# Attention and mixture of experts: V strips and row-sum strips of two steps in one group, a third probabilities buffer, and a token list made by matmuls

## The chip, the cores and the metric

The kernel runs on one core of a Trainium2 chip. The metric is the device time in microseconds of one execution. TensorE multiplies matrices, ScalarE applies functions, VectorE and GpSimd work elementwise, and SyncE (SP) issues transfers. In the profile they are PE (with PEld for its weight loads), ACT, DVE, POOL and SP. SBUF is the memory on the core, PSUM the accumulators of TensorE.

## The reference

The input x has 4 sequences of 1024 tokens with 512 channels. Everything is float32.

```python
q, k, v = (x @ w.T + b, split into 16 heads of 32)
probs = softmax(q @ k.T / sqrt(32))
x = layernorm(x + (probs @ v) @ wo.T + bo)
scores = x @ gate_w.T                       # 8 experts
ew, ei = top_k(scores, 2); ew = softmax(ew)
routed = sum over the two of ew * ((silu(x @ w_gate[e].T) * (x @ w_up[e].T)) @ w_down[e].T)
shared = (silu(x @ sh_gate.T) * (x @ sh_up.T)) @ sh_down.T
x = layernorm(x + routed + sigmoid(x @ se_gate_w.T) * shared)
```

## The kernel before, in words

**Attention.** One sequence is a batch, b of 4; three run in a loop and the last is written out. A batch has 4 groups of 4 heads, and a group has 16 steps: two halves of the queries (512 each) times 8 tiles of keys. `loc` counts the 64 steps of a batch. A step has 4 slots, one for each head. In slot h of step `loc` TensorE computes the scores of step `loc + 1` for head h (`scores`, L549) into a ring of two PSUM banks (`RING`), and ScalarE takes their exponential (`exps`, L683) into a buffer of `probs`. There are two such buffers, chosen by `loc % 2`. At the end of each step TensorE multiplies the probabilities by V (`weighted`, L560): four matmuls with 32 weight columns each, one for each head, which run side by side in the array. These are called strips here. The row sums of the softmax come from `acc`, the sum of the probabilities of two steps (`FOLD`): GpSimd adds the pairs of three heads (L469), VectorE that of the fourth (L795, `FOLD_DVE = 1`), and at every odd step TensorE sums them over partitions with strips (`row_sums`, L574). An exponential waits until its buffer has been multiplied and added.

**Side work.** Each slot also has work for groups further on, given by `side_plan`. "pre" is one of 64 preliminary score matmuls of the next group (L532), of which VectorE takes a row maximum (L765); they use three PSUM banks in a ring. "proj" is one of 16 pieces of the K and Q projection of the group after next: three float32r matmuls of high and low parts (L499). Piece i stands in slot `PROJ_FROM + PROJ_UNIT * (i // 4) + PROJ_EVERY * (i % 4)`, so the last one is in slot 53 of 64. After every fourth piece ScalarE copies the high half (`high`, L663), and VectorE makes the low half ("low", L754) two slots later. "row" sends the maxima back as an extra row of the stacked K and Q.

**Queues.** Each engine works in the order in which the code gives it instructions. SP goes through `body` for each group: inverting row sums, `row` for the first half, weights (`load_w`), for group 1 the next batch's x (`load_x`), `spread`, and `row` for the second half. `spread` (L279) waits for all four low halves of a projection and copies K and Q into `kq_stack` with 12 transfers, three for each head. GpSimd's loop (`batch`) folds at each odd step, normalises at steps 9 and 11, and at step 13 (`SPLIT_W_AFTER`) it first waits for the complete projection and then splits the next weights, which use the same buffer:

```python
if at == SPLIT_W_AFTER and not (last and g > 0):
    projected(b * G + g + 2)      # pool.wait_ge(proj_ready, PROJ * (n + 1))
    split_w(b * G + g + 3)
```

In group 1, step 15 and group 2, steps 1, 3 and 5 it also splits two chunks each of the next x. After a batch come the V tiles of the next batch (`v_tile`, L499, which read `wv_hi` and `wv_lo`) and the output tiles (`o_tile`, L591) with their layernorm. The result x2 goes to memory.

**Feed-forward.** `scores` computes the router. `feed_forward` then has 32 tiles of 128 tokens for the shared expert. The first 12 (`COVER`) run while the routing is worked out; their code is written out, without a loop. VectorE ranks the chosen experts (`first_choice`, `second_choice`, `count`, `positions`). Then GpSimd scatters each token's number to its place in a table in memory, with 64 indirect transfers of 128 numbers of 4 bytes (L1321), and SP reads the table back into `who_all` after the base of tile 9. GpSimd gathers the tokens of 72 expert tiles by it (L1331), one after the other. The other 20 shared tiles and the combination follow.

Of the kernel before, what the change touches and what calls it, by code (L numbers as in the profile page):

```python
# [5 lines left out]
ALU = mybir.AluOpType  # L6
ACT = mybir.ActivationFunctionType
AX = mybir.AxisListType
F32 = mybir.dt.float32
# [24 lines left out]
PROJ_FROM, PROJ_EVERY, PROJ_UNIT = 2, 3, 14  # L34
# [6 lines left out]
FOLD_DVE = 1  # L41
# [46 lines left out]
def attention(nc, x, xT, wkqT, wvT, woT, bq, bk, bv, bo, x2, passed):  # L88

    inv_rows = nc.dram_tensor("inv_rows", (HG, HALF), F32, kind="Internal").ap()  # L90

    with ExitStack() as ctx:
# [16 lines left out]
        wv_hi = sb("wv_hi", [P, C, D], F32R)  # L109
        wv_lo = sb("wv_lo", [P, C, D], F32R)  # L110
# [14 lines left out]
        probs = sb("probs", [P, 2, HG, HALF])  # L125
# [11 lines left out]
        x_nat = probs[:].rearrange("p a h d -> p (a h) d")  # L137
# [47 lines left out]
        wo_in = sem("wo_in")  # L185
        few_in = sem("few_in")
# [14 lines left out]

        def res_of(t):

            return x_nat[:, t - 2, :] if 2 <= t < 6 else res[:, t % 2, :]
# [43 lines left out]
        def _(sp):  # L248
# [62 lines left out]
            def body(b, m, g, last):  # L311
# [57 lines left out]
            spread(0, 0)  # L369
            row(-1, -1, 0, False)  # L370
# [15 lines left out]
        def _(pool):  # L386
# [71 lines left out]
            def fold(b, loc):  # L458

                i, j = loc // FOLD, loc % FOLD  # L460
                for h in range(FOLD_POOL):
# [5 lines left out]
                    if j > 1:  # L467
                        pool.wait_ge(folded, (b * FOLDS + folds(loc) - 2) * FOLD_POOL + h + 1)
                    nc.gpsimd.tensor_tensor(acc[:, h, :], probs[:, (loc - 1) % 2, h, :] if j == 1 else acc[:, h, :],  # L469
                                            probs[:, loc % 2, h, :], ALU.add).then_inc(folded, 1)  # L470
# [24 lines left out]
        def _(pe):  # L495
# [57 lines left out]
            def weighted(b, loc):  # L553
# [5 lines left out]
                for h in range(HG):  # L559
                    done = nc.tensor.matmul(ps_ctx[h * HD:(h + 1) * HD, :],  # L560
                                            v_sb[:, kt, (g * HG + h) * HD:(g * HG + h + 1) * HD],
                                            probs[:, loc % 2, h, :], start=kt == 0, stop=kt == KT - 1)
# [32 lines left out]
            def batch(b, last):  # L595
                for loc in range(BSTEPS):
                    g = loc // STEPS
                    for slot in range(SLOTS):
                        if loc + 1 < BSTEPS:
                            scores(b, loc + 1, slot)  # L600
                        if loc == 0 and slot < SIDE_RING:
                            pe.wait_ge(tail_free, b * TAIL + KT - (2 - slot if slot < 2 else 0) - (slot < 2))
# [25 lines left out]
            with pe.Fori(0, B - 1) as b:  # L628
                batch(b, False)
                pe.wait_ge(side_free, base_of(b * G + G))  # L630
                for t in range(KT):
                    v_tile(b * TAIL + KT + t, t, ps_side[:, t % TAIL_RING, :], TAIL_RING)
                pe.wait_ge(wo_in, 16 * (b + 1))
                for t in range(KT):
                    if t % (KT // NHALF) == 0:
                        pe.wait_ge(ctx_done, (b + 1) * G * NHALF - (t == 0))
                    o_tile(b * TAIL + 2 * KT + t, t, ps_side[:, (KT + t) % TAIL_RING, :],
# [1251 lines left out]
```

## Time and profile before

| | |
|---|---|
| median of 3 runs | 2303.1 us (2297.88 to 2305.36) |
| the profiled execution | 2299.8 us |
| its span, first to last instruction | 2298.1 us |
| mean granted clock of TensorE | 0.972 |
| PE busy | 2130.9 us, 93% |
| PEld busy | 1177.7 us, 51% |
| DVE busy | 1212.6 us, 53% |
| ACT busy | 851.8 us, 37% |
| POOL busy | 953.1 us, 41% |
| attention: first strips of V, first output tile of the last batch | 92.24 us, 1392.71 us |
| shared tiles under the routing | 1494.15 us to 1671.48 us |

Times of instructions count from the start of the span. Busy is the time in which an engine has an instruction at work. A matmul's record is longer than its share of the array, since matmuls overlap, so the distance between starts says what one costs. The granted clock is given as a share of the full 2.4 GHz, and 0.50 is the lower level of 1.2 GHz. Idle time is put down to what ended it; "issue" means that the profile shows nothing that the engine waited for.

### The profile page before, as it was taken

The numbers are of one execution on the slowest core, as the hardware profiler recorded it, in microseconds if no ns is written. First come the engines' busy times: TensorE is split into PE (matmuls) and PEld (weight loads), VectorE is DVE, ScalarE is ACT, GpSimd is POOL, SyncE is SP. The second block draws the span as 40 slices with busy tenths as digits, with TensorE's granted clock in tenths as the row PEclk, the third lists the DMA queues.
The fourth block names the chain that finished last, engine by engine and source line by source line (L and its number), as shares of the span: only waits on it lengthen the run. The fifth ranks groups of instructions, "written<-read, shape, count | busy, mean of one in ns | idle before, by whom it ended". The sixth has DMA issues, their size and how long they took to land. (4 is left out here: it accounts for less than half of the span.)

```text
span 2298.1 us, 34596 instructions
## 1 busy us (share of the span) xinstructions
PE 2130.9 (93%) x9524; PEld 1177.7 (51%) x9525; DVE 1212.6 (53%) x2169; ACT 851.8 (37%) x1508; POOL 953.1 (41%) x926
## 2 busy tenths in 40 slices
PE   7999999999999999999999986791899999999997
PEld 5544445445445445445555422470754444445886
DVE  6767665567665566665567723450222222223875
ACT  2355553355553355554355662320111111111332
POOL 1245753454753454754454564427021111112651
PEclk9999999999999999999999998895999999999999
DMA  4230333221433221333221303560132222223762
GB/s 137 65 71 29 94 70 89 80 61 30 100 68 93 80 48 42 98 70 76 95 55 26 75 11 111 197 256 0 53 105 90 91 90 84 90 91 116 228 184 77
DMA packets 96850, 202.83 MB, mean 88 GB/s; under 512 B 26912, under 2 KB 27424, under 8 KB 94752
## 3 DMA queue, kind: packets, MB, share of 16 engines
q1 hardware_dynamic: 83744, 165.04, 24.6%
q0 software_dynamic: 12928, 35.70, 5.7%
q8 instruction: 78, 1.28, 0.2%
q14 instruction: 100, 0.82, 0.1%
HBM read 110.68 MB, written 39.13 MB: 65 GB/s over the span
## 5 line engine op out<-in xcount | busy, mean ns | idle before, releaser
L765 DVE TENSOR_REDUCE max_half<-ps_side 128x1 f32<-128x512 f32 x1024 | 663.5, 683 | 335.4 <-PE ps_side L532 326.1
L683 ACT ACTIVATE probs<-ps_s 128x512 f32<-128x512 f32 x1024 | 573.4, 596 | 485.9 <-PE ps_s L549 391.2
L469 POOL TENSOR_TENSOR acc<-probs 128x512 f32<-128x512 f32 x384 | 484.7, 1289 | 486.5 <-ACT probs L683 480.8
L549 PE MATMUL ps_s<-kq_stack 97*128 97x512 f32 x1024 | 461.5, 454 | 23.5 <-ACT probs L683 14.4
L532 PE MATMUL ps_side<-kq_stack 96*128 96x512 f32 x1024 | 399.8, 401 | 10.9 <-DVE max_half L765 7.2
L549 PEld LDWEIGHTS ps_s<-kq_stack 97*128 97x128 f32 x1024 | 192.6, 189 | 361.0 <-ACT probs L683 222.3
L560 PE MATMUL ps_ctx<-probs,v_sb 128*32 128x512 f32 x2048 | 274.5, 608 | 0.0
L1433 PE MATMUL ps_gu<-gu_sb,xT_e 128*128 x576 | 261.3, 596 | 0.5 <-issue 0.3
L1331 POOL DMA_INDIRECT x_g<-x,who_all x72 | 67.8, 941 | 389.0 <-PE ps_t L1423 325.7
L532 PEld LDWEIGHTS ps_side<-kq_stack 96*128 96x128 f32 x1024 | 195.9, 191 | 44.9 <-DVE max_half L765 13.8
L1433 PEld LDWEIGHTS ps_gu<-gu_sb,xT_e 128*128 128x128 f32 x576 | 103.7, 190 | 107.7 <-issue 107.3
L1541 ACT ACTIVATE act_g<-ps_gu 128x256 f32<-128x256 f32 x72 | 27.6, 383 | 351.3 <-PE ps_gu L1433 351.3
L1618 DVE TENSOR_TENSOR hid<-act_g,ps_gu 128x256 f32<-128x256 f32 x72 | 30.3, 421 | 224.6 <-ACT act_g L1541 224.6
L1456 PE MATMUL ps_d<-wd_sb,act_g 128*128 x288 | 135.6, 593 | 0.5 <-DVE act_g L1625 0.5
L574 PE MATMUL ps_sum<-acc,ones 128*32 128x512 f32 x1024 | 133.5, 593 | 2.7 <-POOL acc L469 1.4
L795 DVE TENSOR_TENSOR acc<-probs 128x512 f32<-128x512 f32 x128 | 105.7, 826 | 36.8 <-ACT probs L683 36.8
L499 PE MATMUL ps_side<-x_hi,wkq_hi 128*128 128x512 f32 x256 | 103.9, 406 | 15.3 <-DVE x_lo L838 10.7
L1375 PE MATMUL ps_gu<-sgu_hi,xT_hi 128*128 128x512 f32 x256 | 105.0, 410 | 12.8 <-issue 10.4
L499 PE MATMUL ps_side<-x_hi,wkq_lo 128*128 128x512 f32 x256 | 102.3, 400 | 0.0
L499 PE MATMUL ps_side<-x_lo,wkq_hi 128*128 128x512 f32 x256 | 102.0, 399 | 0.0
L1375 PE MATMUL ps_gu<-sgu_hi,xT_lo 128*128 128x512 f32 x256 | 101.7, 397 | 0.3 <-issue 0.3
L1375 PE MATMUL ps_gu<-sgu_lo,xT_hi 128*128 128x512 f32 x256 | 101.5, 396 | 0.0
(194 smaller groups left out, 2477.5 us busy)
## 6 DMA issues: line engine op xcount, KB each, us to landing
kq_stack<-kq SPq DMA_DIRECT2D x192, 256.0 KB, 5.1
y_slots<-y_t SPq DMA_DIRECT2D x72, 256.0 KB, 2.3
res<-inv_rows SPq DMA_DIRECT2D x128, 64.0 KB, 2.0
probs<-x SPq DMA_DIRECT2D x16, 512.0 KB, 5.1
x_r<-x SPq DMA_DIRECT2D x32, 256.0 KB, 3.7
x_t<-x SPq DMA_DIRECT2D x32, 256.0 KB
gu_sb<-wgu SPq DMA_DIRECT2D x8, 1024.0 KB, 14.9
out<-gu_sb SPq DMA_DIRECT2D x32, 256.0 KB, 2.6
```

Of the source, the lines that this page charges most:

```text
L469: nc.gpsimd.tensor_tensor(acc[:, h, :], probs[:, (loc - 1) % 2, h, :] if j == 1 else acc[:, h, :], probs[:, loc % 2, h, :], ALU.add).then_ ...
L499: done = nc.tensor.matmul(out, w, m, start=first and i == 0, stop=last and i == 2)
L532: nc.tensor.matmul(bank, q_stack[par][0:3 * HD, h, t * P:(t + 1) * P], k_stack[par][0:3 * HD, h, half * HALF:(half + 1) * HALF], start=Tru ...
L549: nc.tensor.matmul(ps_s[:, (loc * HG + h) % RING, :], k_stack[par][0:3 * HD + 1, h, kt * P:(kt + 1) * P], q_stack[par][0:3 * HD + 1, h, ha ...
L560: done = nc.tensor.matmul(ps_ctx[h * HD:(h + 1) * HD, :], v_sb[:, kt, (g * HG + h) * HD:(g * HG + h + 1) * HD], probs[:, loc % 2, h, :], s ...
L574: done = nc.tensor.matmul(ps_sum[h * HD:(h + 1) * HD, :], ones[:], acc[:, h, :], start=kt == FOLD - 1, stop=kt == KT - 1)
L683: nc.scalar.activation(probs[:, loc % 2, h, :], ps_s[:, (loc * HG + h) % RING, :], ACT.Exp, scale=HD ** -0.5).then_inc(probs_ready, 1)
L765: nc.vector.reduce_max(max_half[:, u // 2, u % 2:u % 2 + 1], bank, AX.X).then_inc(side_free, 1)
L795: nc.vector.tensor_tensor(acc[:, h, :], probs[:, (loc - 1) % 2, h, :] if j == 1 else acc[:, h, :], probs[:, loc % 2, h, :], ALU.add).then_ ...
L1375: done = nc.tensor.matmul(out, w, m, start=c == 0 and i == 0, stop=c == last_c and i == 2)
L1433: done = nc.tensor.matmul(ps_gu[:, s % 2, :], e_xT[:, s % 2, c, :], gu_sb[:, bass.ds(e, 1), c, :].rearrange("p a n -> p (a n)"), start=c = ...
L1456: done = nc.tensor.matmul(ps_d[:, s % 2, :], e_hT[:, s % 2, c, :], wd_sb[:, bass.ds(e, 1), c, :].rearrange("p a n -> p (a n)"), start=c == ...
```

## The change

Four things are changed together.

1. `weighted` for both steps of a pair and `row_sums` run one after the other at the end of the odd step. A third probabilities buffer, `probs_mid`, takes the steps with `loc % 3 == 1`; an exponential waits for the V strips and the row sums that read its buffer three steps before.
2. `probs_mid` lies on top of `wv_lo` in SBUF. So `wv_lo` is copied to memory once at the start (`wv_lo_kept`), and SP loads it again (1 MB) in the last group of each batch but the last. The V tiles wait for this.
3. GpSimd adds the pairs of all four heads (`FOLD_DVE = 0`), VectorE none. The projection pieces stand in slots 0, 4, 8, ..., 60. The PSUM banks of the tail's tiles are shifted by one.
4. The token table is no longer scattered to memory. VectorE makes one-hot tiles of each token's row in its tile (`in_tile`, 128 columns) and of its tile's number times the token's number (`of_tile`, 72 columns), in 8 parts after tiles 3 to 6. TensorE multiplies them in 64 f32 matmuls that accumulate in `ps_who`, after tiles 4 to 7, and VectorE copies the result to `who_all`.

```diff
-PROJ_FROM, PROJ_EVERY, PROJ_UNIT = 2, 3, 14
+PROJ_FROM, PROJ_EVERY, PROJ_UNIT = 0, 4, 16
-FOLD_DVE = 1
+PROBS = 3
+FOLD_DVE = 0
...
+        with nc.sbuf_tensor("probs_mid", [P, HG, HALF], F32) as probs_mid:
+            pass
         wv_lo = sb("wv_lo", [P, C, D], F32R)
...
+        def probs(loc, h):
+            return probs_mid[:, h, :] if loc % PROBS == 1 else probs_outer[:, loc % PROBS // 2, h, :]
...
+        def tail_bank(i):
+            return ps_side[:, (i + SIDE_RING) % TAIL_RING, :]
         def res_of(t):
-            return x_nat[:, t - 2, :] if 2 <= t < 6 else res[:, t % 2, :]
+            return probs_mid[:, t - 2, :] if 2 <= t < 6 else res[:, t % 2, :]
...
         # SP, body(), after spread
+                if not last and g == G - 1:
+                    sp.wait_ge(pv_done, (b + 1) * BSTEPS - FOLD)
+                    sp.wait_ge(sum_done, (b + 1) * SUMS - 1)
+                    sp.sem_inc(passed_sp, 1)
+                    sp.dma_start(wv_lo[:].bitcast(F32), wv_lo_kept).then_inc(wv_moved, 16)
...
         # SP, at the start
             spread(0, 0)
+            sp.wait_ge(wv_split, C)
+            sp.dma_start(wv_lo_kept, wv_lo[:].bitcast(F32)).then_inc(wv_moved, 16)
...
         # PE, batch()
-                        if slot == SLOTS - 1:
-                            weighted(b, loc)
-                            if loc % FOLD == FOLD - 1:
-                                row_sums(b, loc)
+                        if slot == SLOTS - 1 and loc % FOLD == FOLD - 1:
+                            for done in range(loc - FOLD + 1, loc + 1):
+                                weighted(b, done)
+                            row_sums(b, loc)
...
         # PE, ahead of the V tiles
+                pe.wait_ge(wv_moved, 16 * (b + 2))
...
         # ACT, exps()
-                if loc >= 2:
-                    act.wait_ge(pv_done, b * BSTEPS + loc - 1)
-                    if h < FOLD_POOL:
-                        act.wait_ge(folded, (b * FOLDS + folds(loc - 2) - 1) * FOLD_POOL + h + 1)
-                    else:
-                        act.wait_ge(folded_dve, (b * FOLDS + folds(loc - 2) - 1) * FOLD_DVE + h - FOLD_POOL + 1)
+                if loc >= PROBS:
+                    act.wait_ge(pv_done, b * BSTEPS + loc - PROBS + 1)
+                    act.wait_ge(sum_done, b * SUMS + (loc - PROBS) // FOLD + 1)
...
         # feed_forward
+TABLE_PARTS = 8
+PART = 2 * TT // TABLE_PARTS
+COUNT_COLUMNS_AFTER = 3
+TABLE_AFTER = {3: (0, 1), 4: (2, 3), 5: (4, 5), 6: (6, 7)}
+LOOK_UP_AFTER = {4: (0, 1), 5: (2, 3), 6: (4, 5), 7: (6, 7)}
+WHO_AFTER = 7
...
-            for t in range(TT):
-                for v in range(2):
-                    nc.gpsimd.indirect_dma_start(
-                        table, bass.IndirectOffsetOnAxis(ap=col_i[4][:, v, t:t + 1].bitcast(U32), axis=0),
-                        token[:, t:t + 1], None).then_inc(scattered, 16)
...
+            def look_up(part):
+                pe.wait_ge(part_made, part + 1)
+                for c in range(PART):
+                    done = nc.tensor.matmul(ps_who, in_tile[:, part % 2, c, :], of_tile[:, part % 2, c, :],
+                                            start=part == 0 and c == 0, stop=part == TABLE_PARTS - 1 and c == PART - 1)
+                done.then_inc(part_read, 1)
...
+            def table_part(part):
+                k, first = part * PART // TT, part * PART % TT
+                if part == 0:
+                    dve.wait_ge(columns_made, 1)
+                    link(v.tensor_copy(columns, ps_count))
+                if part >= 2:
+                    dve.wait_ge(part_read, part - 1)
+                v.tensor_tensor(in_tile[:, part % 2], rows[:, 0, k, first:first + PART].unsqueeze(2).broadcast_to((P, PART, P)),
+                                columns.unsqueeze(1).broadcast_to((P, PART, P)), ALU.is_equal)
+                for c in range(PART):
+                    t = first + c
+                    done = v.tensor_scalar(of_tile[:, part % 2, c, :], columns[:, 0:NT], rows[:, 1, k, t:t + 1],
+                                           col[0][:, t:t + 1], ALU.is_equal, ALU.mult)
+                done.then_inc(part_made, 1)
```

## Rows read from the trace of the kernel before

**Rows 1.** Groups of instructions by line: busy, mean ns, idle before by releaser.
```profile
L683 ACT ACTIVATE probs<-ps_s 128x512 f32<-128x512 f32 x1024 | 573.4, 596 | 485.9 <-PE ps_s L549 391.2 <-DVE acc L795 33.9 <-POOL acc L469 23.6
```

**Rows 2.** Timeline of TensorE, last batch's last group: start, us, instruction, idle before.
```profile
1345.58 1.07 PE L560 MATMUL ps_ctx<-probs,v_sb 128*32 128x512 f32 x8
1346.47 1.04 PE L574 MATMUL ps_sum<-acc,ones 128*32 128x512 f32 x8
1347.44 0.73 PE L549 MATMUL ps_s<-kq_stack 97*128 97x512 f32 x2
...
1349.55 1.07 PE L560 MATMUL ps_ctx<-probs,v_sb 128*32 128x512 f32 x8
1350.54 0.73 PE L549 MATMUL ps_s<-kq_stack 97*128 97x512 f32 x2
1351.73 0.99 PE L549 MATMUL ps_s<-kq_stack 97*128 97x512 f32 x2 [0.45 <-ACT probs L683]
1352.65 0.64 PE L560 MATMUL ps_ctx<-probs,v_sb 128*32 128x512 f32 x4
```

**Rows 3.** Timeline of TensorE: first V strips of groups 1 and 2, third batch.
```profile
861.47 1.06 PE L560 MATMUL ps_ctx<-probs,v_sb 128*32 128x512 f32 x8
...
934.67 1.06 PE L560 MATMUL ps_ctx<-probs,v_sb 128*32 128x512 f32 x8
```

**Rows 4.** Timeline of all engines at the end of group 1, second batch.
```profile
572.11 0.97 POOL L403 CAST wkq_hi<-stage 128x512 fp32r<-128x512 f32 x1 [1.12 <-PE ps_side L499]
...
576.33 3.75 POOL L469 TENSOR_TENSOR acc<-probs 128x512 f32<-128x512 f32 x3
...
578.04 0.50 PE L549 MATMUL ps_s<-kq_stack 97*128 97x512 f32 x1
...
580.41 1.07 PE L560 MATMUL ps_ctx<-probs,v_sb 128*32 128x512 f32 x8
```

**Rows 5.** Timelines at the first batch's end; DMA issues: KB each, us to landing.
```profile
374.23 13.78 SPq L279 DMA_DIRECT2D kq_stack<-kq  x12
...
377.08 0.49 PE L532 MATMUL ps_side<-kq_stack 96*128 96x512 f32 x1
...
380.80 0.50 PE L499 MATMUL ps_side<-wv_hi,x_hi 128*128 128x512 f32 x1
381.13 0.40 PE L499 MATMUL ps_side<-wv_hi,x_lo 128*128 128x512 f32 x1
381.37 0.40 PE L499 MATMUL ps_side<-wv_lo,x_hi 128*128 128x512 f32 x1
...
kq_stack<-kq SPq DMA_DIRECT2D x192, 256.0 KB, 5.1
...
acc<-woT SPq DMA_DIRECT2D x3, 1024.0 KB, 5.0
```

**Rows 6.** Windows (busy by engine, PEclk, DMA share, GB/s), timeline; second batch's start.
```profile
438.00:444.00 6.00, 6.00 (x17) 3.22 (x18) 3.65 (x6) 1.19 (x2) 3.46 (x3) 0.50 0.01 4
...
441.54 0.60 ACT L683 ACTIVATE probs<-ps_s 128x512 f32<-128x512 f32 x1 [5.03 <-POOL acc L469]
```

**Rows 7.** Shared tiles: scatter's line, TensorE's timeline, DMA queues 1549 to 1600, window.
```profile
L1321 POOL DMA_INDIRECT table<-token,col_i x64: 954/958/1236, 1532.2 to 1612.0; - x64
...
1549.32 0.60 PE L1369 MATMUL ps_t<-ident_m,x_t 128*128 128x128 f32 x4
1551.37 0.47 PE L1375 MATMUL ps_d<-sd_hi,hT_hi 128*128 128x512 f32 x1 [1.45 <-issue]
...
1613.67 0.76 PE L1375 MATMUL ps_gu<-sgu_hi,xT_hi 128*128 128x512 f32 x1 [10.14 <-issue]
...
1659.65 0.60 PE L1369 MATMUL ps_t<-ident_m,x_t 128*128 128x128 f32 x4
...
1663.20 0.48 PE L1375 MATMUL ps_gu<-sgu_hi,xT_hi 128*128 128x512 f32 x1
...
q0 software_dynamic: 1312, 0.02, 1.9%
q1 hardware_dynamic: 143, 0.26, 1.7%
...
1614.00:1672.00 58.00, 57.00 (x261) 46.30 (x261) 15.99 (x24) 9.63 (x17) 2.96 (x4) 0.96 0.20 63
```

More of the change, by code:

```diff
@@ L185, in attention @@
         wo_in = sem("wo_in")
+        wv_moved = sem("wv_moved")
         few_in = sem("few_in")
@@ L468, in fold @@
                         pool.wait_ge(folded, (b * FOLDS + folds(loc) - 2) * FOLD_POOL + h + 1)
-                    nc.gpsimd.tensor_tensor(acc[:, h, :], probs[:, (loc - 1) % 2, h, :] if j == 1 else acc[:, h, :],
-                                            probs[:, loc % 2, h, :], ALU.add).then_inc(folded, 1)
+                    nc.gpsimd.tensor_tensor(acc[:, h, :], probs(loc - 1, h) if j == 1 else acc[:, h, :],
+                                            probs(loc, h), ALU.add).then_inc(folded, 1)
             def batch(b, last):
@@ L794, in fold @@
                         dve.wait_ge(folded_dve, (b * FOLDS + folds(loc) - 2) * FOLD_DVE + h - FOLD_POOL + 1)
-                    nc.vector.tensor_tensor(acc[:, h, :], probs[:, (loc - 1) % 2, h, :] if j == 1 else acc[:, h, :],
-                                            probs[:, loc % 2, h, :], ALU.add).then_inc(folded_dve, 1)
+                    nc.vector.tensor_tensor(acc[:, h, :], probs(loc - 1, h) if j == 1 else acc[:, h, :],
+                                            probs(loc, h), ALU.add).then_inc(folded_dve, 1)
             def batch(b, last):
@@ L1100, in feed_forward @@
 def feed_forward(nc, x2, sgu_hi, sgu_lo, sd_hi, sd_lo, wgu, wd, base, y, gu_sb, wd_sb, route, sgate_all, weights, pos,
-                 tile_expert, table, ident, out, passed):
+                 tile_expert, ident, out, passed):
     with ExitStack() as ctx:
@@ L1150, in feed_forward @@
         te = spare[:, 0:NT]
+        columns = spare[:, 3 * NT * E + 4 * TT:3 * NT * E + 4 * TT + P]
+        in_tile = x_g[:].rearrange("p s d -> p (s d)").rearrange("p (i c m) -> p i c m", i=2, c=PART)
+        of_tile = spare[:, NT * E:NT * E + 2 * PART * NT].rearrange("p (i c n) -> p i c n", i=2, c=PART)
         y_g = gu_sb[:, 0:4, 0:2, :]
@@ L1257, in _ @@
                 load_tile(t)
-            sp.wait_ge(made, 5)
-            sp.dma_start(table.rearrange("(p n) a -> p (n a)", p=P), zero_table[:]).then_inc(zeroed, 16)
             for e in range(E):
@@ L1484, in _ @@
                 if t == 1:
-                    pe.wait_ge(made, 6)
+                    pe.wait_ge(made, 5)
                     pe.wait_ge(visits, 1)
@@ L1489, in _ @@
                     nc.tensor.matmul(ps_total, all_ones[:], flat, start=True, stop=True).then_inc(counted, 1)
+                if t == COUNT_COLUMNS_AFTER:
+                    pe.wait_ge(ranked, 1)
+                    nc.tensor.matmul(ps_count, all_ones[:], tri[:], start=True, stop=True).then_inc(columns_made, 1)
+                for part in LOOK_UP_AFTER.get(t, ()):
+                    look_up(part)
             expert_turn(0, 0)
@@ L1760, in positions @@
                 link(v.tensor_copy(rows[:, 1], col_i[1][:]))
-                link(v.scalar_tensor_tensor(out=rows[:, 0], in0=rows[:, 0], scalar=float(NT), in1=rows[:, 1],
-                                            op0=ALU.mult, op1=ALU.add))
-                v.tensor_copy(col_i[4][:], rows[:, 0]).then_inc(placed, 1)
-                dve.wait_ge(placed, 1)
+                link(v.tensor_copy(col[0][:], token[:]))
                 link(v.tensor_tensor(ends, tile_start, end[:].unsqueeze(1).broadcast_to((P, NT, E)), ALU.is_ge))
@@ L1785, in _ @@
                     positions(running)
+                for part in TABLE_AFTER.get(t, ()):
+                    table_part(part)
+                if t == WHO_AFTER:
+                    who()
             finish(COVER - 1)
@@ L1809, in moe @@
     y = nc.dram_tensor("y_slots", (SLOTS_ALL, D), F32, kind="Internal").ap()
-    table = nc.dram_tensor("table", (SLOTS_ALL, 1), I32, kind="Internal").ap()
     with ExitStack() as ctx:
@@ L1837, in moe @@
         feed_forward(nc, x2, sgu_hi, sgu_lo, sd_hi, sd_lo, wgu, wd, base, y, gu_sb, wd_sb, route, sgate_all, weights,
-                     pos, tile_expert, table, ident, out, passed)
+                     pos, tile_expert, ident, out, passed)
 def build(nc, x, xT, wkqT, wvT, woT, bq, bk, bv, bo, shg, shu, shd, rw, wgu, wd, out):
```

65 lines of the change are left out of this document (34 added, 31 removed).

## The prediction, made before the changed kernel was run

> **What bounds the kernel now.** I read the page's busy shares, then the idle time by releaser, then the order of instructions at four places. TensorE is busy 93% of the span, so the attention part (to 1393 us) changes only by what changes TensorE's own stream. ScalarE's exponentials wait for TensorE most of the time, and 33.9 + 23.6 us of their idle time ends with an addition into `acc` [rows 1]. Those waits exist because there are two probabilities buffers. In a group with no side work the stream is: strips of one step 0.99 us (1349.55 to 1350.54), strips of V to strips of row sums 0.89, row sums to the next scores 0.97, and 1.19 us for two scores, because the third score waits for the first exponential (a ring of two banks) [rows 2]. A group with projections takes 73.2 us for 16 steps [rows 3], 9.15 us for two.
>
> The feed-forward part has a hole. From 1532.2 to 1612.0 GpSimd issues the 64 scatters of the token table. From 1551 on TensorE's matmuls come singly, and the one at 1613.67 follows 10.14 us of idle time that nothing in the profile explains [rows 7]. The step after `turn` comes 3.55 us later where nothing disturbs (1659.65 to 1663.20). After the `turn` at 1549.32 it was due at 1552.87, and it came 60.8 us late [rows 7].
>
> **The change, part by part.**
>
> *Strips of two steps in one group.* An exit from strips costs 0.99 − 0.89 = 0.10 us, and one of two goes. But ScalarE can work off only two exponentials during a strip group, so the ring of two now paces eight scores in a row instead of twice four. In a bare group: three rounds of 1.19, then 0.92 from the last round to the strips (1351.73 to 1352.65), then 0.89 + 0.89 + 0.97, which is 7.24 us against 7.07 for the pair from 1345.58 to 1352.65 [rows 2]: a loss of 0.17. With projections: 22 matmuls at 0.24 (381.13 to 381.37 [rows 5]) are 5.2, the first after strips adds 0.1 (0.33 instead of 0.24 [rows 5]), strips 2.75. Slots without a projection piece last 0.48 on TensorE and about 0.6 in the ring; I take 0.3 a step for what the slot with a piece doesn't give back, and 0.3 a pair for the copy of a finished projection, which pushes exponentials back. Sum 8.95, against 9.05 (9.15 less the one wait for `kq_stack` in that group, estimated at 1.1 over eight pairs). So −0.1 on 112 pairs: **−11 us**. Bounds: ring free, −0.95 a pair, −106; the bare group's +0.17 on all 128, +22. I stay near the middle rows because rounds of 1.19 stand in the trace with nothing else waited for. The 57.5 us of ScalarE's waits [rows 1] are inside this term.
>
> *GpSimd adds four heads.* Three additions take 3.75 us [rows 4], 1.25 each, so four take 5.0 of a pair's 9: hidden, unless GpSimd starts late. It does at the end of each group. `PROJ_FROM, PROJ_EVERY, PROJ_UNIT` = 0, 4, 16 moves the last projection piece from slot 53 to slot 60. GpSimd's `projected` ahead of `split_w` waits for it, and the fold of steps 14 and 15 is queued behind. Count from the score of slot 60 (578.04 [rows 4]): the piece ends at +1.4, the split lasts 4.2 (572.11 to 576.33), four additions 5.0: sums ready at +10.7. TensorE's strips started at +2.37 (580.41); a piece (0.7) and the copy (0.2) more give +3.3, two V strips 1.76: row sums wanted at +5.1. TensorE stands for **5.6 us**, and ScalarE's `take` and the next scores' exponentials stand with it. This happens where `split_w` follows and no larger wait covers it: groups 0 to 2 of three batches and group 0 of the last, 10 × 5.6 = **+56** (bounds 4.5 and 6.5 each). Before, three additions were ready in time.
>
> *Clock.* After the idle time at a batch's start the granted clock was 0.50 from 438 to 444 [rows 6], the lower level, 1.2 GHz. After each 5.6 us I take some 3.4 us at that level, half of which is lost: 10 × 1.7 = **+17** (bounds 0 and 34).
>
> *The reload of `wv_lo`.* It is behind `spread` in SP's queue. `spread` now waits for the low half at slot 62: copy and subtraction after the piece bring it to +3.1 after slot 60, where before it started before slot 60 (374.23 against 377.08). Its 12 transfers take SP 13.8 us, so the reload is issued at +17. The last transfers land about 5.1 us after their issue, and 1 MB lands 5.0 after its own on quiet queues [rows 5]: between +22 and +25, taken +23.5. TensorE reached the first V tile at +3.7 (380.80); with a second step's strips it is +4.6. It waits 18.9 us, three times: **+57**, and +2 each for the clock, **+6**. The row sums' wait of that group lies under it. The inversion of the last row sums and the loads of x follow the reload in SP's queue, but the V tiles (96 matmuls at 0.24) take 23 us and start late as well, so they stay covered; if not, it costs a few us a batch.
>
> *`spread` elsewhere.* Its first head lands 6.5 after the start (1.4 for three issues, 5.1 to land), at +9.6; the next group's first preliminary scores want it at +6.4. Where the row sums wait it is hidden; the last batch's group 1 pays 3, and in group 1 of the others it is behind `load_x`, which waits for the split: 1 each. **+6.** *x splits:* pairs with four additions and two split chunks (5.0 + 4.2 + gaps) need 9.4 on GpSimd against 8.95, in four pairs of three batches: **+6** (0 to 15). *Batch start:* the first strips and the wait of 5.03 us on `acc` at 441.54 [rows 6] go, while TensorE's wait for VectorE after its loop turns stays: **−7** (0 to −12). *Prologue:* the same later last piece, and the copy of `wv_lo` out: **+3** (0 to 8).
>
> *Token list by matmuls.* The scatters go, the hole with them: 60.8, plus 3.4 for the slow matmuls after it and 0.6 in the next step: **−65**. The price is 64 f32 matmuls of two passes. The nearest row is four transposes of 128 columns in 0.60, the last alone 0.27, so 0.11 a pass: 128 × 0.11 = **+14**, on TensorE's path (bounds: 8, if columns alone count, and 31 at the 0.24 of a 512-column matmul). VectorE was busy 16 of 58 us in this stretch at 0.67 an instruction [rows 7], so its new work, some 3 us a part and two parts a tile, lies beside TensorE's 9.1 + 3.5. At 0.67 for each narrow one too it would show, by up to 13 us.
>
> Against this stands a rule. No packet of an instruction queue is among those of 1549 to 1600 [rows 7]. By the Trainium skill, Runtime: NRT & Kernel Launch, "Instruction fetch mechanics", fetching is mostly hidden in code without taken branches, and this stretch is unrolled; the trace agrees that no fetch was under way. By that rule removing scatters cures no lack of instructions, and unless they block something else the hole would stay.
>
> **Sum.** −11 + 56 + 17 + 57 + 6 + 6 + 6 − 7 + 3 = +133 in attention; −65 + 14 = −51 after it; together +82 on the profiled execution's 2299.8, 2382. The median of the runs is 3.3 above that execution: **2385 us**.
>
> **The rivals.**
> 1. *The ring costs nothing* (the other side). If TensorE's path in a pair is only its matmuls, a pair is 8.1, −95 more: 2290. It decides when the eight scores lose under 0.1 us a pair to exponentials. For it: ScalarE is busy 37%. Against: the rounds of 1.19 [rows 2] don't depend on that share.
> 2. *The row sums don't wait*: the fold of four is ready by +5.1. Then 56 and 17 go and `spread` shows at nine more ends, +27: 2339. Against: the order in GpSimd's queue.
> 3. *The hole stays*, being no effect of the scatters: 2450. Against: it lies inside them and ends with them.
> 4. *The reload is covered* (it lands by +4.6, ahead of the spread): −63, 2322. Against: the queue's order.
>
> **How the numbers follow.** Forecast 0.70, with its own range 2335 to 2430; rival 1: 0.11; rival 2: 0.08; rival 3: 0.05; rival 4: 0.06. The range of 8 in 10 runs from 2318 to 2435: it takes in rivals 2 and 4 and leaves out 1 and 3. A difference of 0.3% is what a measurement of this kernel can tell. Slower 0.85; faster 0.11, nearly all of it rival 1; within 0.3% 0.04, between rivals 1 and 4.
>
> **What would show it.** A wait of the row sums' matmuls on `acc` of 5 to 6 us at 10 group ends; waits of the first V tiles for `wv_lo`, three of nearly 19 us; a granted clock below 1 after both; score waits for exponentials in nearly every pair; a closed hole in the feed-forward part, with 0.1 us for each pass of the look-up. The forecast is wrong if waits at group ends stay under 2 us, if the reload lands before the strips end, or if GpSimd's four additions take much more than 5.0 and every pair waits for them.

## The result and the profile after

The changed kernel took 2373.8 us, the median of four runs from 2370.0 to 2385.5, against 2303.4 for the kernel before: a ratio of 1.032 (interval 1.028 to 1.036). It is slower by 70 us where 82 were forecast. Its profiled execution spans 2372.0 us at a mean granted clock of 0.954, where before had 2298.1 and 0.972.

I read the waits of TensorE first. Columns: engine and line, what it waited for, us in total, times, the longest.

```profile
PE ps_sum L595 <- POOL acc L490: 73.7, 14, 6.2
PE ps_side L520 <- DMA wv_lo<-wv_lo_kept: 38.7, 3, 13.2
PE ps_s L570 <- ACT probs_outer L705: 20.9, 52, 0.8
...
PE ps_s L570 <- ACT probs_mid L705: 11.5, 26, 0.8
...
PE ps_side L553 <- DMA kq_stack<-kq: 6.5, 2, 3.9
```

The first two rows are the two waits of the forecast: 14 on GpSimd's additions (ten of 5.3 us at the group ends, three of 6.15 at the batch ends and one of 2.2 at the end of the last batch) and 3 on the reload. The scores' waits for exponentials are 78, 32.4 us in all; the forecast looked for one in nearly every pair, and from 99 to 1316 us, 104 pairs, there are 49. Before, ScalarE's exponentials had 485.9 us of idle time ahead of them, 33.9 and 23.6 of it for an addition into `acc` [rows 1]. After, the view of the exponentials' line gives what ended their idle time (us, times):

```profile
its engine sat idle before it (us, times) until:
  PE ps_s L570: 409.3, 291
  issue: 0.9, 3
```

No addition is among the releasers. What is left is waiting for TensorE, and making it shorter would not make TensorE's own work shorter. Here is why the row sums wait: GpSimd's timeline at the end of group 1 of the second batch, which answers to [rows 4].

```profile
619.89 0.61 POOL L424 CAST wkq_hi<-stage 128x512 fp32r<-128x512 f32 x1 [6.62 <-PE ps_side L520]
...
622.49 1.27 POOL L426 TENSOR_TENSOR wkq_lo<-stage,wkq_hi 128x512 fp32r<-128x512 f32 x1
623.72 4.91 POOL L490 TENSOR_TENSOR acc<-probs_outer,probs_mid 128x512 f32<-128x512 f32 x4
```

TensorE's timeline of the same place, with the last projection piece at its head:

```profile
618.78 0.40 PE L520 MATMUL ps_side<-x_hi,wkq_hi 128*128 128x512 f32 x1
...
621.44 1.06 PE L581 MATMUL ps_ctx<-probs_outer,v_sb 128*32 128x512 f32 x8
622.32 1.04 PE L581 MATMUL ps_ctx<-probs_mid,v_sb 128*32 128x512 f32 x8
628.69 1.94 PE L595 MATMUL ps_sum<-acc,ones 128*32 128x512 f32 x8 [5.32 <-POOL acc L490]
```

GpSimd has been idle for 6.62 us when the last piece lets it go on; then the split and the four additions follow, and the row sums start 0.06 us after the last addition (623.72 + 4.91). The fold has nothing to do with the piece; it is only queued behind the split that waits for it. The row-sum matmuls take 1.94 instead of 1.04 us, because the clock fell during the wait (windows; columns after the length are PE, PEld, DVE, ACT and POOL busy, the granted clock, DMA share and GB/s):

```profile
620.00:624.00 4.00, 2.56 (x19) 0.67 (x18) 1.04 (x3) 2.50 (x5) 3.84 (x5) 1.00 0.20 60
624.00:632.00 8.00, 3.31 (x11) 1.18 (x12) 0.00 (x0) 1.11 (x3) 7.84 (x8) 0.65 0.82 184
```

At the first batch's end, [rows 5] before, SP's queue and then TensorE's:

```profile
396.16 14.13 SPq L293 DMA_DIRECT2D kq_stack<-kq  x12
410.93 0.66 SPq L346 DMA_DIRECT2D wv_lo<-wv_lo_kept  x1
```

```profile
403.40 1.94 PE L595 MATMUL ps_sum<-acc,ones 128*32 128x512 f32 x8 [6.15 <-POOL acc L490]
418.59 0.79 PE L520 MATMUL ps_side<-wv_hi,x_hi 128*128 128x512 f32 x1 [13.24 <-DMA wv_lo<-wv_lo_kept]
```

The reload is issued once the 12 transfers of `spread` are out, and it lands 7.6 us after its issue. TensorE stands for 6.15 + 13.24 = 19.4 us at this batch end, and about as long at the other two (the three waits for `wv_lo` are 38.7 us in all), and from 402 to 422 us it had half its clock:

```profile
402.00:422.00 20.00, 5.35 (x17) 2.95 (x18) 0.00 (x0) 0.60 (x1) 1.35 (x2) 0.51 0.83 218
```

How long the groups are can be read from the first V strips of groups 0, 1, 2 and 3 of the third batch and of group 0 of the last batch:

```profile
862.88 0.64 PE L581 MATMUL ps_ctx<-probs_outer,v_sb 128*32 128x512 f32 x4
941.35 0.64 PE L581 MATMUL ps_ctx<-probs_mid,v_sb 128*32 128x512 f32 x4
1020.01 1.06 PE L581 MATMUL ps_ctx<-probs_outer,v_sb 128*32 128x512 f32 x8
1098.41 0.64 PE L581 MATMUL ps_ctx<-probs_outer,v_sb 128*32 128x512 f32 x4
1241.03 1.06 PE L581 MATMUL ps_ctx<-probs_outer,v_sb 128*32 128x512 f32 x7
```

Group 1 takes 78.7 us where it had 73.2 [rows 3]. Group 0 takes 78.5 us, and the group that ends the batch 142.6 us with V and output tiles. Before, these two took 72.2 and 123.2 us, from the V strips of the second step of groups 0, 1 and 3 and of the last batch's group 0 (the second step, because it is the one that ends a pair):

```profile
793.05 0.64 PE L560 MATMUL ps_ctx<-probs,v_sb 128*32 128x512 f32 x4
...
865.24 1.06 PE L560 MATMUL ps_ctx<-probs,v_sb 128*32 128x512 f32 x8
...
1013.51 0.64 PE L560 MATMUL ps_ctx<-probs,v_sb 128*32 128x512 f32 x4
...
1136.67 0.64 PE L560 MATMUL ps_ctx<-probs,v_sb 128*32 128x512 f32 x4
```

A pair of the last group, without projections ([rows 2] before: 7.07 us):

```profile
1465.14 1.92 PE L581 MATMUL ps_ctx<-probs_outer,v_sb 128*32 128x512 f32 x16
1466.91 1.06 PE L595 MATMUL ps_sum<-acc,ones 128*32 128x512 f32 x8
1467.91 0.73 PE L570 MATMUL ps_s<-kq_stack 97*128 97x512 f32 x2
1469.09 0.99 PE L570 MATMUL ps_s<-kq_stack 97*128 97x512 f32 x2 [0.45 <-ACT probs_outer L705]
1470.28 0.99 PE L570 MATMUL ps_s<-kq_stack 97*128 97x512 f32 x2 [0.19 <-ACT probs_outer L705]
1471.46 1.00 PE L570 MATMUL ps_s<-kq_stack 97*128 97x512 f32 x2 [0.19 <-ACT probs_outer L705]
1472.39 1.06 PE L581 MATMUL ps_ctx<-probs_mid,v_sb 128*32 128x512 f32 x8
```

From strips to strips it takes 7.25 us, with three score rounds of 1.19 in a row, as worked out ahead. In the feed-forward part the hole is closed: TensorE has no idle time from 1673 to 1740 us (window below). The look-up's 128 passes come in four sets of 32. With such a set the next matmul follows 3.93 us after the transposes (1666.88 to 1670.81), where without one it follows after 0.35 (run 9, 1553.32 to 1553.67): 3.58 us a set, 0.11 us a pass.

```profile
1666.88 0.60 PE L1418 MATMUL ps_hts<-ident_m,hid 128*128 128x128 f32 x4
1667.32 3.69 PE L1483 MATMUL ps_hts<-y_t,x_g 128*128 128x72 f32 x32
1670.81 0.48 PE L1393 MATMUL ps_gu<-sgu_hi,xT_hi 128*128 128x512 f32 x1
```

```profile
1673.00:1740.00 67.00, 67.00 (x369) 57.38 (x368) 30.87 (x70) 10.12 (x18) 4.04 (x4) 1.00 0.20 63
```

The first output tile of the last batch comes at 1519.07 us against 1392.71: +126.4 for attention (+133 forecast). The profiled execution is longer by 2373.8 − 2299.8 = 74.0, so −52.4 is left for everything after (−51 forecast).

### The profile page after: what moved, and what is told of

Read it like the earlier page. It is cut to its first block and busy times, and to the rows that moved or that the text cites. A ratio compares the mean times of both kernels' runs of the same rounds, so it can differ in the third digit from the quotient of the medians.

```text
span 2372.0 us, 34378 instructions
## 1 busy us (share of the span) xinstructions
PE 2149.6 (91%) x9654; PEld 1216.2 (51%) x9655; DVE 1140.7 (48%) x2114; ACT 854.6 (36%) x1508; POOL 1036.6 (44%) x989
## 5 line engine op out<-in xcount | busy, mean ns | idle before, releaser
L787 DVE TENSOR_REDUCE max_half<-ps_side 128x1 f32<-128x512 f32 x1024 | 648.4, 683 | 457.7 <-PE ps_side L553 450.3
L705 ACT ACTIVATE probs_outer<-ps_s 128x512 f32<-128x512 f32 x688 | 389.1, 596 | 289.1 <-PE ps_s L570 268.6
L553 PE MATMUL ps_side<-kq_stack 96*128 96x512 f32 x1024 | 404.9, 407 | 14.4 <-DVE max_half L787 7.7
L490 POOL TENSOR_TENSOR acc<-probs_outer,probs_mid 128x512 f32<-128x512 f32 x176 | 220.2, 1282 | 123.0 <-ACT probs_mid L705 116.9
L490 POOL TENSOR_TENSOR acc<-probs_outer 128x512 f32<-128x512 f32 x176 | 220.0, 1280 | 116.7 <-ACT probs_outer L705 116.7
L490 POOL TENSOR_TENSOR acc<-probs_mid,probs_outer 128x512 f32<-128x512 f32 x160 | 200.4, 1284 | 117.2 <-ACT probs_outer L705 117.2
L705 ACT ACTIVATE probs_mid<-ps_s 128x512 f32<-128x512 f32 x336 | 191.0, 596 | 149.3 <-PE ps_s L570 140.7
L595 PE MATMUL ps_sum<-acc,ones 128*32 128x512 f32 x1024 | 146.4, 646 | 73.7 <-POOL acc L490 73.7
L581 PE MATMUL ps_ctx<-probs_outer,v_sb 128*32 128x512 f32 x1376 | 177.0, 610 | 0.0
L595 PEld LDWEIGHTS ps_sum<-acc,ones 128*32 128x32 f32 x1024 | 32.4, 114 | 157.7 <-POOL acc L490 96.0
```

Of the source, the lines that this page charges most:

```text
L490: nc.gpsimd.tensor_tensor(acc[:, h, :], probs(loc - 1, h) if j == 1 else acc[:, h, :], probs(loc, h), ALU.add).then_inc(folded, 1)
L553: nc.tensor.matmul(bank, q_stack[par][0:3 * HD, h, t * P:(t + 1) * P], k_stack[par][0:3 * HD, h, half * HALF:(half + 1) * HALF], start=Tru ...
L581: done = nc.tensor.matmul(ps_ctx[h * HD:(h + 1) * HD, :], v_sb[:, kt, (g * HG + h) * HD:(g * HG + h + 1) * HD], probs(loc, h), start=kt == ...
L595: done = nc.tensor.matmul(ps_sum[h * HD:(h + 1) * HD, :], ones[:], acc[:, h, :], start=kt == FOLD - 1, stop=kt == KT - 1)
L705: nc.scalar.activation(probs(loc, h), ps_s[:, (loc * HG + h) % RING, :], ACT.Exp, scale=HD ** -0.5).then_inc(probs_ready, 1)
L787: nc.vector.reduce_max(max_half[:, u // 2, u % 2:u % 2 + 1], bank, AX.X).then_inc(side_free, 1)
```

## The experiments

Each was timed beside the kernel before on its own chip. The first four ran on a chip where the kernel before took 2301.2 us (median of 11), the other eight on one where it took 2246.2 and 2246.0 us (23 and 16 runs). Which chip the runs of the result were made on isn't on record; their times and the hole in the trace of before are those of the first of these two, and they are counted with it. What makes the two chips differ became a question of its own (runs 7 and 9 to 12).

**1. The fold ahead of the split.** The split moves behind the last pair's fold.

```diff
-NORM_AFTER, SPLIT_W_AFTER = (11, 9), 13
+NORM_AFTER, SPLIT_W_AFTER = (11, 9), 15
```

> The changed kernel with the weights' split moved from step 13 to step 15 of a group, so that GpSimd adds the last pair before it waits for the projection piece of slot 60. My theory (the order in GpSimd's queue makes the row sums wait): the ten waits of 5.3 us on acc go; what then shows is spread's late landing, which the last batch's group 1 shows already (last pair 12.6 us there, 16.1 where the row sums wait, 8.8 with neither). So 3.6 us at ten ends, about -36: 2338 us, with waits on kq_stack of 3 to 4 us in place of those on acc, and the first V tiles' wait for wv_lo longer by 6 us. Rival (four additions on GpSimd are simply too much work, whatever their order): the row sums still wait, some 2374 us.

Measured: 2366.0 us, ratio 1.029 (1.026 to 1.032), so 8 us less than the change and not 36. The cause was right and the gain was not. The waits of TensorE:

```profile
PE ps_side L520 <- DMA wv_lo<-wv_lo_kept: 59.7, 3, 20.3
PE ps_side L553 <- DMA kq_stack<-kq: 51.5, 12, 8.6
```

No row sum at the end of a group with projections waits for `acc` any more. But the next group's first preliminary score now waits for `spread`, and the whole of the batch end's 20 us is a wait for the reload. At the first group end (TensorE's timeline):

```profile
164.26 0.50 PE L570 MATMUL ps_s<-kq_stack 97*128 97x512 f32 x1
167.59 0.50 PE L553 MATMUL ps_side<-kq_stack 96*128 96x512 f32 x1 [2.83 <-DMA kq_stack<-kq]
```

In group 1 that wait is longer than the one it replaces, because SP issues x loads ahead of `spread` there, and they wait for the split, which now comes later still (the first batch's group 1):

```profile
248.26 0.79 PE L553 MATMUL ps_side<-kq_stack 96*128 96x512 f32 x1 [8.30 <-DMA kq_stack<-kq]
```

So the first batch's group 1 became 3.5 us longer than in the changed kernel (81.9 against 78.4), while its groups 0 and 2 became 2.9 and 3.3 shorter (V strips to V strips in the two traces). The three waits lie one above the other, and all three start later because the last projection piece is in slot 60. For the reload that is the smaller part, as run 2 shows.

**2. The reload ahead of `spread`** in SP's queue (in `body`).

```diff
+                if not last and g == G - 1:
+                    ...
+                    sp.dma_start(wv_lo[:].bitcast(F32), wv_lo_kept).then_inc(wv_moved, 16)
                 if not (last and g >= G - 2):
                     spread(m + 2, g % 2, m, ...)
```

> The changed kernel with the reload of wv_lo ahead of spread in SP's queue (it still waits for the strips of step 61). My theory (the reload is late because it is queued behind spread's 12 transfers): the three waits of V tiles (13.2 us each) go, and with them some 4 us each at the lower clock; the row sums' wait of that end stays. -17 a batch, -51: 2323 us. Rival (the reload is late because of its own length, or its wait for the strips): V tiles still wait over 5 us each, 2350 or more.

Measured: 2334.1 us, ratio 1.015 (1.012 to 1.017). The wait for `wv_lo` is gone from the list, the one on `acc` is unchanged at 73.7 us, and the change loses 40 of its 70 us. The reload was late by the order in the queue, not by its 1 MB, and not by the projection piece, which stood in slot 60 here too. The expected 2323 was missed by 11 us: it had 51 us for the three waits, and they gave 40.

**3. Both together.**

> Both moves together. My theory: neither wait is left at the batch ends, -19 each, and -36 at the ten other group ends: 2281 us, 1% faster than the kernel before, all of it from the token list. Rival (one of the two waits hides a third thing, for instance the row sums' inversion or the loads of x behind spread in SP's queue): the batch ends stay above 75 us and the total above 2300.

Measured: 2308.7 us, ratio 1.0037 (1.0025 to 1.0049). The total stays above 2300, as the rival said, and the expected 2281 was missed by 28 us. Without the reload's wait above it, moving the split is worth 25 us. What is left is the third wait:

```profile
PE ps_side L553 <- DMA kq_stack<-kq: 51.8, 12, 8.6
```

**4. The new token list alone**: attention as before, the feed-forward part as changed.

```diff
-                    nc.gpsimd.indirect_dma_start(
-                        table, bass.IndirectOffsetOnAxis(ap=col_i[4][:, v, t:t + 1].bitcast(U32), axis=0),
-                        token[:, t:t + 1], None).then_inc(scattered, 16)
+LOOK_UP_AFTER = {4: (0, 1), 5: (2, 3), 6: (4, 5), 7: (6, 7)}
```

> The attention part of the kernel before with the feed-forward part of the changed one: the token list by matmuls alone. My theory (the scatters block every engine for some 60 us): -65 for the hole and +14 for 128 passes of 0.11 us, 2252 us (2247 to 2258). Rival (the hole comes from something else in this stretch): it stays, and the look-ups add their 14: 2317 us.

Measured: 2247.9 us, ratio 0.977 (0.975 to 0.979). On this chip the list is worth −53 us, as in the changed kernel, and TensorE has no idle time in the hole's place (window):

```profile
1548.00:1614.00 66.00, 66.00 (x364) 56.57 (x363) 30.20 (x68) 10.12 (x18) 4.04 (x4) 1.00 0.21 64
```

From here on the kernel before takes 2246 us.

**5. The reload first, and the projection pieces in their old slots**, two moves at once, so that all three waits should go. The reload stands ahead of `spread` as in run 2; the second edit is this.

```diff
-PROJ_FROM, PROJ_EVERY, PROJ_UNIT = 0, 4, 16
+PROJ_FROM, PROJ_EVERY, PROJ_UNIT = 2, 3, 14
```

> The changed kernel with the reload of wv_lo ahead of spread and the projection pieces back in their old slots (2, 3, 14: the last in slot 53); the split is at step 13 as before. My theory (all group-end waits come from the piece in slot 60): no wait on acc, on kq_stack or on wv_lo over 1.5 us is left; pairs keep their 8.9 us against 9.05, so attention gains some 15 us, and with the list's 54 the kernel takes 2303 - 54 - 15 + 3 for the start = 2237 us. Rival (four additions and the split are too much for GpSimd at a group's end even so): the row sums wait some 2 us at each end, clock included 2270.

Measured: 2254.4 us, ratio 1.0046 (1.003 to 1.0062). In its trace no V tile waits for the reload of `wv_lo`, preliminary scores wait three times for `kq_stack` (2.8 us in all), and the row sums wait once for `acc`, 2.2 us at the end of the last batch. The 17 us missed are not a matter of the chip: 2303 less the list's 54 is 2249 us, and the list alone took 2247.9 and 2245.8 us on the two chips. What isn't there is the gain of 15 us in attention; run 12 shows where it is lost. No run has the pieces in their old slots with the reload still behind `spread`. By the rows of before, `spread` would then be out at 388.0 us (374.23 + 13.78), the reload would land some 7.5 us later, as it does in the changed kernel, and the V tiles would want it at about 381.7 (380.80 and 0.9 for a second step's strips): a wait of some 14 us, an estimate. So the slot alone would not have cured the reload.

**6. The same with each step's V strips in a group of their own.**

```diff
-                        if slot == SLOTS - 1 and loc % FOLD == FOLD - 1:
-                            for done in range(loc - FOLD + 1, loc + 1):
-                                weighted(b, done)
-                            row_sums(b, loc)
+                        if slot == SLOTS - 1:
+                            weighted(b, loc)
+                            if loc % FOLD == FOLD - 1:
+                                row_sums(b, loc)
```

> As the one with the pieces in the old slots, and besides the strips of each step in a group of their own, as before the change; third buffer, four additions and list stay. It gives what joining two steps' strips is worth. My theory (0.10 to 0.20 us a pair saved on entries and exits, most of it lost again to the ring of two score banks, which gets only two exponentials done under a strip group): within 10 us of the joined one, either side; the third buffer alone gives most of the attention's gain. Rival (joining is worth its full 0.2 us on 128 pairs): 26 us slower than the joined one.

Measured: 2251.5 us, ratio 1.0028 (1.0017 to 1.0038). Merging the strips gains nothing; the version with the strips apart is 0.1% faster, and the intervals overlap. By the traces merging gives 0.4 us in each group 0 (71.6 us in run 5, 72.0 here), and in a bare group it costs (7.25 us a pair, where before had 7.07).

**7. Half the scatters** in the kernel before. This version leaves out the second choice of each token, so it is of use for its times alone.

```diff
-                    sp.wait_ge(scattered, 16 * 2 * TT)
+                    sp.wait_ge(scattered, 16 * TT)
...
-                for v in range(2):
+                for v in range(1):
```

> The kernel before with 32 scatters instead of 64 (the second choice of each token is not entered in the table; the gathers then fetch token 0 for it, at the same sizes). If the scatters block the engines from a point some 14 to 17 of them after the first until the last is issued, the hole ends 32 x 1.26 = 40 us sooner: 2263 us. If the hole is a fixed effect of this stretch, it keeps its 60 us: 2303.

Measured: 2231.2 us, ratio 0.994 (0.992 to 0.996). Neither theory said this: this chip has no hole to halve. The 15 us are another matter, told with run 9.

**8. Pieces every four slots, but 14 slots a unit.**

```diff
-PROJ_FROM, PROJ_EVERY, PROJ_UNIT = 0, 4, 16
+PROJ_FROM, PROJ_EVERY, PROJ_UNIT = 0, 4, 14
```

> The changed kernel with the reload ahead of spread and the pieces in slots 0, 4, 8, 12 of units 14 apart (the last in slot 54). The two end waits depend on the last piece alone, so it should be within 5 us of the one with the old slots: 2237. Rival (evenly spread pieces matter for the ring: a piece in slot 0 of each step gives exponentials time): 10 us or more apart.

Measured: 2377.3 us, ratio 1.058 (1.056 to 1.060), a miss by 140 us. The waits of TensorE:

```profile
PE ps_side L520 <- DVE kq L776: 65.6, 42, 1.8
PE ps_side L520 <- POOL x_lo L426: 26.3, 8, 4.9
```

The last piece of a unit is in slot 12, VectorE makes its low half two slots on, in slot 14, and there the next unit's first piece already wants the bank: 1.6 us, 42 times. Slots 0, 4, 8, 12 of 16 leave room; 2, 5, 8, 11 of 14 as well. The placement of the pieces is a matter of single slots. The two rows are 78 us more than in run 5, of the 123 us between the two runs; the rest isn't accounted for, and a part may be the clock (0.953 granted against 0.981).

**9. The kernel before again, for its trace on this chip.**

> The kernel before, unchanged, for its trace on the chip of this call. On the chip of the second call it took 2246.2 us where the first two calls had 2303.4 and 2301.2, and with half of the scatters 2231.2. If the stretch without tensor work beside the 64 scatters (62.3 us on the first chip) belongs to the chip and not to the program, this trace has it where the time is near 2302 and doesn't have it where the time is near 2246, with all other stretches alike. If it is always there, a time near 2246 must show some 55 us less in other stretches, the attention's above all.

Measured: 2248.8 us. Attention is the same (the last output tile starts at 1422.3 us against 1421.5), and the hole isn't there. Windows, to be read beside those of the kernel before at the same stretch, which follow in a second fence:

```profile
1548.00:1614.00 66.00, 60.08 (x291) 49.60 (x289) 18.52 (x27) 11.32 (x20) 49.94 (x53) 0.99 0.17 49
```

```profile
1548.00:1614.00 66.00, 9.01 (x28) 5.18 (x27) 2.07 (x3) 1.79 (x3) 49.44 (x52) 0.54 0.04 8
```

The scatters are the same in both, 64 from 1533.0 to 1612.8 us at 958 ns here [rows 7 for before]. What does show here is a wait that the hole had hidden: the first expert tile wants its tokens, and they can't be gathered until the last scatter is done and the table read back.

```profile
1621.16 1.12 PE L1423 MATMUL ps_t<-ident_m,x_g 128*128 128x128 f32 x4 [13.08 <-DMA x_g<-x,who_all]
```

With half the scatters, of which the last starts at 1568.5 us, that wait is gone: 15 us less in run 7. The instruction queues among the DMA queues between 1549 and 1600 us in this trace:

```profile
q8 instruction: 2, 0.03, 0.3%
q14 instruction: 2, 0.02, 0.1%
```

In the trace of before the same stretch had no packet of an instruction queue [rows 7]; in that of run 4, on the first chip without scatters, it had three.

**10. The changed kernel again.**

> The changed kernel, unchanged, beside the kernel before on this chip. It has no scatters, so it should take about 2373 us on any chip if the missing hole is what makes the kernel before 57 us faster on the second call's chip: ratio 1.031 where the kernel before takes 2302, 1.057 where it takes 2246. If that chip is faster in other stretches, the changed kernel is faster there too: about 2318 us and a ratio still near 1.03.

Measured: 2376.8 us, ratio 1.058 (1.056 to 1.061), with waits on `acc` of 73.7 us and on `wv_lo` of 38.7 us, as in the trace of the result. The changed kernel is as fast on both chips (2373.8 and 2376.8), and so is the list alone (runs 4 and 11); only the kernel before differs.

**11. The list alone again.**

> The kernel before with the new token list alone (no scatters, look-ups from a table). It took 2247.9 us beside 2301.2. Where the kernel before has its hole: 0.977 again. Where it hasn't: the scatters' own cost is gone, but the look-ups' 14 us are added (four passes of 3.58 us), so within 0.5 per cent of 2246 us, ratio 0.997 to 1.004. If this chip is faster in other stretches, 0.977 on it too, some 2195 us.

Measured: 2245.8 us, ratio 1.0002 (0.9993 to 1.0011). On this chip the list is worth nothing: it saves the 13 us of waiting of run 9 and adds some 14 for the look-up.

**12. Run 5's version beside it.** The edits are those of run 5 and no others.

> The changed kernel with the reload of the weights ahead of the spread, the projection pieces early in each group and the adds begun early (2254.4 us on the second call's chip). It too has no scatters and should take 2250 to 2258 us on any chip; beside the list alone (2247.9 us) it says what the merged strips and GpSimd's adds cost once both waits are gone: some 5 us. If the merged strips are worth their switches (11 us by the prediction), it is the faster of the two.

Measured: 2255.0 us, ratio 1.0038 (1.0023 to 1.0052), 9 us over the list alone. One row of its waits is larger than with the list alone, where `x_lo` costs 5.2 us in six waits:

```profile
PE ps_side L520 <- POOL x_lo L426: 13.4, 6, 3.5
```

It is the stretch in which GpSimd also splits the next x. With four heads to add, it is late. In the traces the groups 2 of the three batches together take 13.3 us more than with the list alone (run 11), of which these waits are 8.2, and the last group takes 6.4 more; the other groups are shorter, by up to 2.1 us. In run 6 the groups 2 are as long (78.8, 78.7 and 79.3 us, against 78.7, 81.2 and 78.1 here and 75.7, 74.2 and 74.8 in run 11), so this is not the work of the merged strips. That it is the fourth addition fits, and no run takes it back by itself.

## Why the prediction was right, and where it wasn't

*The row sums' wait* (10 × 5.6): 5.3 us each, and 6.15 at the three batch ends, where the forecast had counted it under the reload's. From the last piece to the end of the additions the forecast had 9.3 us, and it took 9.0. Run 3 against run 2 prices the order in GpSimd's queue at 25 us net, because `spread` comes next; the prediction's rival 2 had put that cover at 27 of its 73, and it is more like 48 (73 less 25). Run 1 shows the limit of that rival: alone it is worth 8.

*The reload* (57 and 6 for the clock): TensorE stands for 19.4 us at the first batch's end where 18.9 were forecast, and the reload landed 22.4 us after the start of `spread` (20.4 forecast). Run 2 puts its share at 40 us, not 63. The rest is time in which TensorE also waits for the row sums (3 × 6.15), and that wait stays when the reload's goes. So rival 4's price was too high by 23 us; in the sum it makes no difference.

*The clock*: the granted clock falls to its lower level of 1.2 GHz at these waits (0.65 from 624 to 632 us, 0.51 from 402 to 422). The prediction took some 3.4 us at that level after each wait, a choice for which it gave no row. The third batch's group 0 became 6.3 us longer (78.5 against 72.2). Of this 5.3 are the wait; with −0.6 for the strips (next point) 1.6 are the clock (1.7 forecast). The two mean granted clocks, 0.954 and 0.972, would understate it, since the mean of before holds the hole, 66 us at 0.54 in which TensorE had next to nothing to do.

*The strips* (−11, with bounds −106 and +22): the ring does pace eight scores in a row, and the bare pair came out at 7.25 (7.24 forecast). With the waits gone, group 0 of run 12 takes 71.6 us where the list alone has 72.2, −0.6 where −0.8 was forecast. Rival 1 falls. But not all of the 0.6 is the merging: in run 6, with the third buffer and the strips apart, the group takes 72.0. And over the whole kernel run 6 shows no gain: apart is no slower.

*The mis-sized terms*. `x` splits: +6 forecast. In the change's group 2 the next x is split behind longer waits and nothing shows (+3.7 a group, where groups 0 and 1 have +5.3 to +6.3); once these are gone, run 12 waits 8 us more for it than the list alone. The two bare groups at the end stand at nothing in the sum, though the prediction's own 0.17 us a pair would have given 16 pairs 2.7 us. The last one alone has +8.2 to the output tile (0.9 of it because the second step's strips now stand behind the mark from which it is measured). In it the V strips ran twice at half speed, and a window shows the clock at 0.62:

```profile
1479.50:1484.00 4.50, 4.50 (x25) 1.03 (x24) 0.00 (x0) 1.48 (x3) 1.82 (x2) 0.62 0.01 4
```

No wait of note stands ahead of it; the bare group before had 1.00 throughout. What made it fall isn't shown. The sum over attention was 126.4 where 133 were forecast. That it came so close is in part luck. The ten group ends had 65 us of the forecast (5.6 + 1.7 − 0.8 each), or 71 with the x splits, and these groups became 53.5 us longer in the traces; the two bare groups at the end were left out of the sum and became 9.5 us longer.

*The token list* (−65 and +14): on the first chip −52.4 for −51, and the look-up at 0.11 us a pass, as taken. VectorE's new work stayed hidden (31.2 us busy in the 40 from 1660). But one step of this part is wrong in its reason. The prediction said that the hole is made by the scatters. Run 9 shows the same scatters, in the same kernel, without a hole, and run 11 the list then worth nothing. On the first chip the hole goes when the scatters go (run 4), and they aren't enough to make one. So the ratio is 1.032 on one chip and 1.058 on the other, where the change costs 131 us (run 10). The forecast could not have seen it from one trace; that its −65 held is luck of the chip on which the two were timed.

*The row on instruction fetch*: the prediction took the missing instruction packets as a sign that no fetch was wanted. Where nothing is disturbed, the same 51 us have four of them (run 9). None in the hole can as well mean that fetches were wanted and didn't come, with TensorE, VectorE and ScalarE at a stand at the same time. In the trace of before TensorE is idle for 40.0 us at one place and VectorE for 50.4, both with nothing waited for:

```profile
1602.42 1.11 PE L1400 MATMUL ps_hts<-ident_m,hid 128*128 128x128 f32 x4 [40.00 <-issue]
```

```profile
1601.67 0.69 DVE L1595 TENSOR_TENSOR hid<-act_g,ps_gu 128x512 f32<-128x512 f32 x1 [50.41 <-issue]
```

That reading, in which the scatters kept instruction fetches from being served on one chip, was argued, not shown, as no run changed the fetching, and one thing in the same trace speaks against it. TensorE went on at 1613.67 [rows 7], as the last scatter ended, but from 1600 to 1625 us its DMA queues show no packet of an instruction queue either; the next ones come after that. So the standing ended without a fetch that the trace shows, and through what the scatters held the three engines stays open. The Trainium skill, Runtime: NRT & Kernel Launch, "Instruction fetch mechanics", says that crossing a block boundary is mostly hidden in straight code; run 9 agrees, with four packets and no hole. If fetching is what failed in the trace of before, its 60.8 us are a case that the rule does not foresee; if not, the rule has no part in the hole.

## What to carry to other kernels

Look for what a late instruction has queued behind it on its engine: here one projection piece, moved from slot 53 to 60, held a split, a fold, a copy and, in part, a reload, and a wait removed alone uncovered the next (8 us, 40 us, together 65). Price such waits as a stack, not as a sum. Free the cause that they share, and ask of each whether it has one of its own as well, as the reload had in its place behind 12 transfers. And where idle time ends on nothing that the profile shows, time the kernel on another chip before counting its removal as a gain.

## What the runs showed of the hardware

On one chip 64 indirect scatters of 128 numbers each (954 ns of GpSimd's time each) went with some 60 us in which three engines issued next to nothing; on another the same code lost none of it and the kernel was 2.5% faster, 2246 against 2303 us. These are two chips, and no run tells what differs between them. A float32 matmul of 72 columns costs 0.11 us a pass. The best complete version here for both chips is the kernel before with the list by matmuls: 2247.9 us on the first and 2245.8 us on the second, faster than before on one and the same within the interval on the other.
